# A two-element attention and soft-MoE layer: every weight slab streamed as float32 with its casts on GpSimd, and attention scores issued in waves of eight key tiles

## The reference

```python
# attention: 16 heads of 128, 4 key/value heads, rope on q and k
q, k, v = x @ wq, x @ wk, x @ wv
scores = einsum('bhqd,bhkd->bhqk', q, k) / sqrt(128)
p_g = softmax(where(causal, scores, neg))      # all keys up to the query
p_l = softmax(where(local,  scores, neg))      # a window of 256
x = layernorm(x + (0.5 * (p_g @ v + p_l @ v)) @ wo)

# soft mixture of experts: 16 experts, 128 slots each, hidden 512
x_ln    = layernorm(x) * gamma + beta
logits  = l2norm(x_ln) * scale @ l2norm(mu)
slot_in = x_ln^T @ softmax(logits, over tokens)
h       = gelu(slot_in @ W1 + b1)
y       = combine(softmax(logits, over slots), h @ W2 + b2)
x = layernorm(x + y)
```

## Time and profile before

| | us |
|---|---|
| median of 2 runs | 10078.62 |
| lowest, highest | 10012.99, 10144.25 |
| profiled execution, its own time | 10134.66 |
| its span (first to last instruction, core 3) | 10132.9 |
| spans of its 8 cores | 10043.6 to 10132.9 |

### The profile page before, as it was taken

The page is one execution under the profiler, slowest core; times in us unless marked ns, Lnnn a source line. Parts: engine busy times, 40 slices in busy tenths (PEclk is TensorE's granted clock), DMA queues, the critical chain, the costliest instruction groups (busy, mean ns, idle before and its releaser), DMA issues.

```text
span 10132.9 us, 78161 instructions; the slowest of 8 cores (10043.6 to 10132.9 us)
## 1 busy us (share of the span) xinstructions
PE 6226.9 (61%) x21410; PEld 2260.3 (22%) x21410; DVE 2408.2 (24%) x4039; ACT 2177.9 (21%) x4678; POOL 468.9 (5%) x636
## 2 busy tenths in 40 slices
PE   4665665656395665553384666556565766667777
PEld 1211111111132232221031211111111222223223
DVE  1223223233232220001121233333323332200012
ACT  1122112112133321111121122222212232322212
POOL 1000000000100111112300000000000000000000
PEclk8666566566586666665596666666666767777768
DMA  4000000000333224446723000000000230111232
GB/s 131 10 13 7 13 13 10 10 13 6 100 124 116 91 68 140 125 129 205 232 107 116 5 3 5 5 5 3 5 5 3 91 130 32 42 69 59 71 129 112
DMA packets 180015, 645.14 MB, mean 64 GB/s; under 512 B 21327, under 2 KB 21328, under 8 KB 163192
## 3 DMA queue, kind: packets, MB, share of 16 engines
q1 hardware_dynamic: 133784, 451.37, 15.1%
q0 software_dynamic: 32000, 104.88, 2.6%
q10 hardware_dynamic: 13824, 83.89, 2.0%
HBM read 451.31 MB, written 188.74 MB: 63 GB/s over the span
## 4 chain that ended last, share of the span: by engine, by line
PE 47%; DVE 19%; DMA 16%; ACT 9%; issue 7%; DVEq 1%; SPq 0%; ACTq 0%
PE pb L314 47%; ACT AR L325 6%; DMA AR<-W 6%; DVE AR L620 4%; DVE AR L621 4%; DMA AR<-x 2%; DMA AR<-xT 2%; DVE AR L297 1%; DMA AR<-x1sp 1%; DMA AR<-wbc 1%; ACT AR L323 1%; DMA x1sp<-AR 1%; DMA out<-AR 1%; DMA AR<-wo 1%; DVE AR L375 1%
## 5 line engine op out<-in xcount | busy, mean ns | idle before, releaser
L314 PE MATMUL pb<-AR 128*128 128x512 bf16 (+6 forms) x21410 | 6226.9, 435 | 3874.4 <-DVE AR L621 908.2
L314 PEld LDWEIGHTS pb<-AR 128*128 128x128 bf16 (+2 forms) x21410 | 2260.3, 114 | 7840.4 <-issue 7055.5
L325 ACT ACTIVATE AR<-pb 128x128 bf16<-128x128 f32 (+3 forms) x3360 | 1197.9, 420 | 3249.2 <-PE pb L314 3193.8
L620 DVE RECIPROCAL AR<-pb 1x512 f32<-1x512 f32 x128 | 428.3, 3346 | 246.9 <-PE pb L314 246.9
L565 DVE TENSOR_TENSOR AR<-AR 128x128 bf16<-128x128 bf16 x512 | 115.2, 225 | 1465.0 <-PE pb L314 799.7
L621 DVE RECIPROCAL AR<-pb 1x512 f32<-1x512 f32 x128 | 420.1, 3282 | 0.0
L367 ACT ACTIVATE AR<-pb 64x512 bf16<-64x512 f32 x160 | 95.1, 594 | 1512.2 <-PE pb L314 1497.9
L325 ACT ACTIVATE AR<-AR 128x1 f32<-128x1 f32 (+4 forms) x288 | 257.1, 893 | 681.5 <-DVE AR L943 544.3
L323 ACT ACTIVATE AR<-AR 128x2048 bf16<-128x2048 f32 x96 | 183.3, 1910 | 976.2 <-DVE AR L707 434.4
L297 DVE CAST AR<-AR 128x1024 bf16<-128x1024 f32 x232 | 160.9, 694 | 968.9 <-DMA AR<-W 566.2
L375 DVE TENSOR_TENSOR AR<-pb,AR 128x512 bf16<-128x512 f32 x160 | 110.6, 691 | 1166.6 <-ACT AR L369 1166.6
(11 more groups left out here) (44 smaller groups left out, 1066.9 us busy)
## 6 DMA issues: line engine op xcount, KB each, us to landing
AR<-W SPq DMA_DIRECT2D x256, 512.0 KB, 5.4
wbc<-AR POOLq DMA_DIRECT2D x400, 256.0 KB, 5.1
AR<-wbc SPq DMA_DIRECT2D x200, 512.0 KB, 3.3
AR<-xT SPq DMA_DIRECT2D x64, 512.0 KB, 4.7
AR<-x SPq DMA_DIRECT2D x32, 1024.0 KB, 5.5
x1sp<-AR ACTq DMA_DIRECT2D x32, 1024.0 KB, 3.9
AR<-xlnsp SPq DMA_DIRECT2D x64, 512.0 KB, 4.7
AR<-mu_r SPq DMA_DIRECT2D x64, 512.0 KB, 5.3
```

What stands on the lines that cost most here:

```text
L314: e.matmul(out=o, lhsT=l, rhs=r, start=s, stop=t),
L325: e.activation(out=o, in_=i, func=f, bias=bi, scale=sc)),
L620: vt_op(lambda e: e.reciprocal(out=rrow[0], in_=PB[4].ap()[0:1, :]), inc=False)
```

## The change

Two things change.

Weights: the buffer in DRAM, its stores and its loads are gone, in both elements. `stream2` always loads two float32 halves through `wst0` and `wst1`, and both are cast by POOL; DVE casts none. cos and sin are float32 in DRAM now and are also brought in as four halves through the staging buffers, with a cast on POOL. K projection waits for `wk` alone in both elements (before, in element 1, for `wv` too).

Attention: a query group issues its key tiles in waves of up to eight. All scores of a wave (with their exps and masks) are written first, then the PV and sum matmuls of the wave. The wait for `pb2.free`, `pb4.free` and `vt.rdy` stands behind the first wave's scores, and `ebuf` is freed once a wave. Groups 0 to 3 have 4, 8, 12 and 16 key tiles, so one, one, two and two waves.

```diff
-            dma_in(cosv, d_cs[0], "cosv", sem="D_cs")
-            dma_in(sinv, d_cs[1], "sinv", sem="D_cs")
+            for ti, dstv in ((0, cosv), (1, sinv)):
+                for hf in range(2):
+                    sl = rr[0] % 2
+                    rr[0] += 1
+                    dma_in(wst[sl], d_cs[ti, :, hf * 1024:(hf + 1) * 1024], f"wst{sl}")
+                    p.need("gpsimd", f"wst{sl}.rdy")
+                    p.op("gpsimd", ... tensor_copy(out=dstv[...], in_=wst[sl]), inc=[("Pq", 1)])
...
-        def stream2(dram_ap, dst_bf, nm, cache=True):
-            if cache and cmode[0] == 1:
...
-                p.op("sync", lambda e, d=dst_bf, s=d_wbc[sidx]: e.dma_start(out=d, in_=s),
-                     inc=[(rsem, 16)])
...
+        def stream2(dram_ap, dst_bf, nm):
             for hf in range(2):
                 sl = rr[0] % 2
-                ceng = "gpsimd" if sl == 0 else "vector"
...
                 dma_in(dst_st, src, f"wst{sl}")
-                p.need(ceng, f"wst{sl}.rdy", nm + ".free", nm + ".wc")
-                p.op(ceng, lambda e, d=dst_bf[:, hf * 1024:(hf + 1) * 1024], s=wst[sl]:
-                     e.tensor_copy(out=d, in_=s), inc=[(csem, 1)])
...
-                    p.op("gpsimd", lambda e, d=d_wbc[sidx][:, hf * 1024:(hf + 1) * 1024],
-                         s=dst_bf[:, hf * 1024:(hf + 1) * 1024]: e.dma_start(out=d, in_=s),
-                         inc=[(wsem, 16)])
...
+                p.need("gpsimd", f"wst{sl}.rdy", nm + ".free")
+                p.op("gpsimd", lambda e, d=dst_bf[:, hf * 1024:(hf + 1) * 1024], s=wst[sl]:
+                     e.tensor_copy(out=d, in_=s), inc=[("Pq", 1)])
...
-                    p.need("tensor", "pb2.free", "pb4.free", "vt.rdy")
...
-                    for j in range(jmax + 1):
-                        # score(j); then, for j >= 1, emit_pv(j - 1); then exp(j) and mask
-                    emit_pv(jmax)
+                    for w0 in range(0, jmax + 1, 8):
+                        wave = list(range(w0, min(w0 + 8, jmax + 1)))
+                        for j in wave:
+                            # score(j), exp(j) and mask
+                        if w0 == 0:
+                            p.need("tensor", "pb2.free", "pb4.free", "vt.rdy")
+                        for j in wave:
+                            # PV(j) and sum(j)
+                        twave = p.c("T")
+                        for j in wave:
+                            p.set_tok(f"eb{j % 8}.free", T=twave)
```

More of the change, by code:

```diff
@@ L40, in host_constants @@
     s4 = float(d) ** -0.25
-    cs = np.stack([np.asarray((np.cos(emb).T * s4).astype(np.float16)),
-                   np.asarray((np.sin(emb).T * s4).astype(np.float16))])
+    cs = np.stack([(np.cos(emb).T * s4).astype(np.float32),
+                   (np.sin(emb).T * s4).astype(np.float32)])
     tri = (np.arange(128)[:, None] <= np.arange(128)[None, :]).astype(BF)
@@ L142, in build_program @@
     d_xlnsp = nc.dram_tensor("xlnsp", [T, C], BF16, kind=spkind).ap()
-    d_wbc = nc.dram_tensor("wbc", [200, 128, C], BF16, kind="Internal").ap()
     if debug:
@@ L444, in build_program @@
                 p.barrier()
[L445 to L446 removed]
             if a0stop < 1:
                 continue
[L450 to L452 removed]
+            for ti, dstv in ((0, cosv), (1, sinv)):
[4 more added lines that the diff above has]
+                    p.need("gpsimd", f"wst{sl}.rdy")
+                    p.op("gpsimd", lambda e, d=dstv[:, hf * 1024:(hf + 1) * 1024],
+                         s=wst[sl]: e.tensor_copy(out=d, in_=s), inc=[("Pq", 1)])
+                    p.mark(f"wst{sl}.free", "Pq")
+            p.set_tok("cs.rdy", Pq=p.c("Pq"))
             for cc in range(NCH):
[L454 to L455 removed]
+                stream2(d_xT[el, cc * 128:(cc + 1) * 128, :], xTv[cc], f"xT{cc}")
             if a0stop < 2:
                 continue
[L458 removed]
             for nm, dsrc, slabs in (("wk", d_wk, wkb_slab), ("wv", d_wv, wvb_slab)):
[L460 removed]
                 for q in range(4):
                     ap = dsrc[q * 512:(q + 1) * 512, :].rearrange("(a p) n -> p a n", p=128)
[L463 to L467, removed]
+                    stream2(ap, slabs[q], f"{nm}{q}")
+                p.set_tok(nm + ".rdy", Pq=p.c("Pq"))
             if a0stop < 3:
@@ L479, in build_program @@
                     if kv == 0 and tg == 0:
-                        p.wait("tensor", "D_cs", cstok)
+                        p.need("tensor", "cs.rdy")
                         for cc in range(NCH):
@@ L499, in build_program @@
             p.mark("vt.rdy", "S")
[L501 to L505, removed]
             for h in (HEADS if phases >= 2 else []):
                 kv = h // 4
-                stream2(d_wq[h], wsb[0], "wsbq")
+                tq = stream2(d_wq[h], wsb[0], "wsbq")
                 for tg in range(4):
@@ L929, in build_program @@
                     slw = qd % 2
-                    stream2(ap, wsb[slw], f"wsbF{slw}")
-                    p.need("tensor", f"wsbF{slw}.rdy")
+                    tkw = stream2(ap, wsb[slw], f"wsbF{slw}")
+                    p.wait("tensor", "Pq", tkw)
                     p.wait("tensor", "S", stiT)
@@ L977, in build_program @@
                     slw = hc % 2
-                    stream2(d_w2[e_, hc * 128:(hc + 1) * 128, :], wsb[slw], f"wsbF{slw}")
-                    p.need("tensor", f"wsbF{slw}.rdy")
+                    tkw = stream2(d_w2[e_, hc * 128:(hc + 1) * 128, :], wsb[slw], f"wsbF{slw}")
+                    p.wait("tensor", "Pq", tkw)
                     if hc == 0:
```

122 lines of the change are left out of this document (48 added, 74 removed).

## The result

| | before | after |
|---|---|---|
| median, us | 10076.51 (42 runs) | 10147.71 (43 runs) |
| lowest, highest | 9994.03, 10187.30 | 10071.24, 10229.45 |
| profiled execution, its own time | 10134.66 | 10071.24 |
| its span | 10132.9 | 10069.7 (core 5) |

The changed kernel takes 1.0072 of the time before, 95% interval [1.0052, 1.0093]: about +71 us, where +62 was forecast. It is no difference at the 2% of the forecast, and a small loss by the interval.

What follows compares the result with a forecast made beforehand. No engine was seen near full; weight handling made the elements differ, and attention was the longest stage. Weights -28 (element 0 -325, element 1 +297) plus waves +90 gave +62 us: median 10141, range 10010 to 10330.

Steps and rivals of the forecast that it cites:

- the pace: Weight streaming: a slab takes 6.0 us, the cycle of one staging buffer; bounds 5.8 to 6.9.
- the steps -8, +69, +153, and +22: Stage changes in us: `wo` fill -8 (element 0) and +69 (element 1); element 1's FFN2 +153, its fill and K/V +22.
- The prediction's sentence that no one on the path waited for the stores: Weights: POOL's queue loses its 400 stores of the bfloat16 copy, for which nothing on the path waited.
- The step +53: FFN1 of element 1: slab 3 alone late, +3.3 us per expert over 16 experts, so +53 us.
- two terms for element 0 taken from one core: Element 0's attention (-84 us, a DVE cast behind the head's last DVE operation) and logits (-18 us) become like element 1's.
- the waves: Attention order: net +2.8 us per head, +90 us over 32 heads, after 8.1 per head gained from earlier scores.
- the four steps: Attention, per head: the two first groups -0.2 us each, the third +0.4, the last +2.8.
- The pace of 6.9: Rival on weight streaming: 6.9 us a slab with eight cores loading, +184 us, 10325; chance 0.10.
- the cold clock: Rival in attention: the clock never rises in a wave, pairs stay 0.99 us, +243 us, 10294; chance 0.15.
- the upper clock throughout: Rival in attention: the upper clock holds through the waves, -211 us, 9840; chance 0.08.
- The port rival: Rival in the logits stage: the port lock shared with GpSimd casts hits DVE, 10241 us; chance 0.05.
- The prediction's +100 us: Logits stages: up to 96 added POOL casts of 1.04 us could delay DVE operations; left out of the sum.

Runs made afterwards that it cites:

- the measured pair: Kernel before with the wait for pb2.free, pb4.free, vt.rdy moved behind each group's second score, with old weights (9899.44 us) and with the new weights (9947.61 us).
- the late wait: Kernel before, alternating order kept, its wait for pb2.free, pb4.free and vt.rdy moved behind the group's second score: 9899.44 us, ratio 0.9848.
- the second execution of before: The kernel before run once more, unchanged, for a second trace: 10128.28 us.
- alternating casts: Kernel before without DRAM copies in either element, casts on POOL and DVE in turn, old attention order: 10297.68 us, ratio 1.0249.
- the late wait with all casts on POOL: The late wait with old weights, plus element 0's casts all on POOL, DRAM copies and stores kept: 9758.57 us, ratio 0.9707 to before.

## Why the prediction held, and where it did not

**Held: the pace.** 6.0 us a slab gave 404 for FFN2 and 131 for the `wo` fill; after shows 405 and 402, 132 and 130. Against the measured pair the steps -8, +69, +153, and +22 for the fill of element 1 read -8, +74, +157 and +24. Putting the pace at `xT`'s, the stream with no write-back, rather than at that of FFN2 of element 0 was right: the stores alone bring FFN2 back to 6.8. The prediction's sentence that no one on the path waited for the stores was wrong in effect, since they cost some 115 us of element 0; its terms for FFN1 and FFN2, taken from whole stages, held that price all the same.

**Held: FFN1, with its sequence.** Worked out: 14.9 us from the bias matmul, slab 3 alone late, 672. Measured: 14.2 and 666 and 663. The last late cast was put to end within 13 us of the bias matmul; it ends at 9046.38, 11.9 after it. The step +53 was thus too high: +30.

**Failed: two terms for element 0 taken from one core.** I gave attention -84 and the logits -18, the differences between the elements of core 3, the slowest core of an execution 56 us above the median. With the order left alone, attention in element 0 goes from 2328 and 2321 in two executions to 2270, -55; under the late wait it is -37. The logits of element 0 are 661 in the second execution of before: nothing was to be gained. The rows had said why: the granted clock of that stage is 0.66 in element 0 and 0.76 in element 1, and core 6, at 0.76 in element 0 too, takes 659 us where core 3 takes 679:

```profile
3045.00:3704.00 659.00, 403.91 (x1920) 189.58 (x1952) 157.29 (x246) 205.68 (x303) 73.34 (x96) 0.76 0.29 90
```

The six slower cores of that stage (677 to 681 us) are those whose clock records show 0.81 in it, for 287 to 343 us; the two at 659 and 660 show none. In the second execution the same excess (667 to 678 us) lies in element 1. FFN2 was sized from core 3 as well, but rightly: -57, where the executions of before lie 52 to 58 us over the new weights in the old order, and -44 came in the pair. The mechanism of attention (a cast at the end of a head in DVE's queue) is real: where both elements have it, attention is 2318 and 2315 instead of 2270 and 2268. In one element PE waits 41.6 us for its 15 casts:

```profile
L297 DVE CAST AR<-AR x15: 684/686/687, 5548.9 to 7610.6; 128x1024 bf16<-128x1024 f32 x15
...
  PE pb L314: 41.6, 15
```

So element 0 gains 253 and not 325, element 1 loses 283 and not 297. The sum is +30 (measured +27 and +30) in place of -28: a small difference of two large sums, whose sign the forecast missed. That the total came within 9 us of the measured +71 is luck: this error and that of the waves cancel.

**Mis-sized: the waves.** +2.8 us a head was forecast, +41 / 32 = 1.3 measured. In the last group the parts were 12.3 (first wave), 4.9 (scores), 6.4 and 3.0; the timeline has 11.5 to the end of the first pairs (5973.05 to 5984.56), 4.7 to the second pairs at about 5989.3, and 8.9 to the reciprocal. The clock rose 2.8 us into the pairs, not 4.7. And the forecast's price for the upper level was read where it was not granted in full: the 1.05 us between the sums in the earlier trace rows stand in a stretch at 0.81,

```profile
6325.00:6338.00 13.00, 12.07 (x41) 3.52 (x39) 1.53 (x7) 6.71 (x15) 0.00 (x0) 0.81 0.00 0
```

so that a pair came out at 0.70 where 0.63 is measured at 1.00. The fall in the second wave came as foreseen. By periods the four steps are -0.8, -0.5, +1.7, +0.7 where -0.2, +0.4, +2.8, -0.2 stood. Behind the net stand two larger numbers, and both were put too high: the stall removed is worth 210 us in this order (259 put), and the waves cost 210 + 41 = 251 us (349 put).

**The rivals.** The pace of 6.9 is excluded by 402 us in FFN2, the cold clock by pairs 0.63 apart, the upper clock throughout by those 1.06 apart. The port rival moved no stage, and its DVE operations were not the ones that waited; see below.

**Not settled.** No run here shows how much of the waves' cost is the lower clock of the second wave and how much the idle time of the score phases, and why the clock rises later in the Q projection under the late wait.

## What to carry to other kernels

When a change moves a wait and reorders work at once, cost and try them apart: here the wait alone was one line worth -1.5%, and the waves that brought it gave it all back. Do not put a cast that a load's buffer depends on into the queue of an engine that waits for PE; an idle engine that takes 1.04 us for it beats a busy one that takes 0.69; in stages in which that engine is free, the 0.69 wins again (FFN2, 391 against 405 us). And where the answer is the difference of two sums of 300 us, take the stage times of several cores and executions and compare their granted clocks first, since one core's attention and logits carried some 50 us of a lower clock into it.

## What the runs showed of the hardware

**Of a DVE operation and a GpSimd cast that meet, the one that started first keeps its time and the other waits.** In the logits stage the DVE product of two bfloat16 inputs takes 1.22 us and a POOL cast 1.04. After, the cast starts 0.22 us into the product and takes 1.90 (56 of the 64 products have such a cast beside them):

```profile
3104.66 1.22 DVE L738 TENSOR_TENSOR AR<-AR 128x2048 bf16<-128x2048 bf16 x1
```
```profile
3104.88 1.90 POOL L276 CAST AR<-AR 128x1024 bf16<-128x1024 f32 x1 [13.97 <-DVE AR L768]
```

With alternating casts the POOL cast starts 0.21 us into a DVE cast and 0.65 ahead of the product:

```profile
3120.18 0.69 DVE L297 CAST AR<-AR 128x1024 bf16<-128x1024 f32 x1
...
3120.39 1.37 POOL L297 CAST AR<-AR 128x1024 bf16<-128x1024 f32 x1 [15.57 <-DVE AR L804]
...
3121.04 1.80 DVE L774 TENSOR_TENSOR AR<-AR 128x2048 bf16<-128x2048 bf16 x1 [0.17 <-DVE AR L297]
```

Each time the one that started later is longer by its overlap with the earlier one less about 0.14 us: the cast after by 0.86 for 1.00 of overlap, this product by 0.58 for 0.72, this cast by 0.33 for 0.48 with the DVE cast, and the cast of before by 0.19 for 0.33. That is what comes out if the later one is held until the earlier ends, but for its first 0.14 us. The Trainium skill (SBUF — State Buffer, "Who interferes with whom") says that whoever issues first has the shared port pair for the whole instruction and the other is blocked; the traces agree. The prediction's +100 us took the case in which the DVE operation comes second. After, the product always comes first (its longest of 64 is 1.23 us), so the casts waited, and they had cover. No stage paid in either order: logits take 661 us in both these kernels.

**The granted clock of a dense stretch differs between executions.** The K/V projection of element 1 is the same matmuls in every kernel. By windows, in the first execution of before and after:

```profile
5496.00:5663.00 167.00, 151.39 (x561) 61.27 (x559) 29.05 (x61) 34.57 (x59) 0.00 (x0) 0.79 0.01 4
```
```profile
5185.00:5323.00 138.00, 122.41 (x560) 53.59 (x558) 30.65 (x60) 33.74 (x57) 10.04 (x10) 1.00 0.13 39
```

It takes 167 us at a granted 0.79 and 138 at 1.00. The second execution of before has 168 at 0.79, the new weights in the old order 160 at 0.85, the pair of late waits on which the stage table rests 145 at 0.93 and 145 at 0.94, and the late wait with all casts on POOL 139 at 0.99. Summed over the clock records of the traces, the clock stands at 0.81 for 1479 to 1644 us of every core's span in the first execution of before and for 1027 to 1952 in the second, for none on any core of the kernel after, of the late wait with the new weights or of the alternating casts, and for 0 to 901 in the others. Where in the span it stands changes from core to core and from one execution to the next, as in the logits stage above; what decides it no run here shows. It makes the fills of element 1 differ by +3 and +9 between the two executions of before (278 and 272) and after (281), where the forecast had +22 and the pair has +24, and is the reason not to subtract two of them.
